# Moving GpSimd's two multiplies of the decayed C ahead of the first rotation sum

## The reference

```python
Bm = _rms(Braw, B_norm_w)[:, :, None, :] + B_bias      # per head
Cm = _rms(Craw, C_norm_w)[:, :, None, :] + C_bias
tc = jnp.cumsum(theta, axis=1)
cos_t, sin_t = (jnp.cos(tc), jnp.sin(tc))
def rope(v):
    v1, v2 = (v[..., :N // 2], v[..., N // 2:])
    return jnp.concatenate([v1 * cos_t - v2 * sin_t, v1 * sin_t + v2 * cos_t], -1)
Bm, Cm = (rope(Bm), rope(Cm))
def step(carry, inp):
    h, prevBx = carry
    x_t, B_t, C_t, a_t, g_t, b_t = inp
    Bx = jnp.einsum('bhp,bhn->bhpn', x_t, B_t)
    h = a_t[..., None, None] * h + g_t[..., None, None] * Bx + b_t[..., None, None] * prevBx
    y = jnp.einsum('bhpn,bhn->bhp', h, C_t)
    return ((h, Bx), y)
```

## Time and profile before

| what | value |
|---|---|
| median of 3 runs | 1266.17 us (1259.84 to 1267.21) |
| the profiled execution | 1261.08 us, of which its span is 1259.3 us |
| DVE busy | 1185.8 us, 94% |
| PE busy | 1121.2 us, 89% |
| ACT busy | 820.9 us, 65% |
| POOL busy | 766.8 us, 61% |
| mean granted TensorE clock | 0.963 |

### The profile page before, as it was taken

One profiled execution on the slowest core, in us unless ns is written; L12 is line 12 of the kernel. 1 busy time (PEld: TensorE's weight loads), 2 busy tenths in 40 slices (PEclk: granted clock), 3 DMA queues, 4 the chain that ended last, 5 costly groups with the idle time before them and its releaser, 6 DMA issues. The chain is left out here.

```text
span 1259.3 us, 30431 instructions
## 1 busy us (share of the span) xinstructions
PE 1121.2 (89%) x11442; PEld 819.0 (65%) x11442; DVE 1185.8 (94%) x1795; ACT 820.9 (65%) x1270; POOL 766.8 (61%) x594
## 2 busy tenths in 40 slices
PE   3876489999999999999999999999999999999996
PEld 3753266667667667667666766666776676676665
DVE  7899489999999999999999999999999999999994
ACT  4677256666766676667666666667666666667663
POOL 4002146766766667666776676666766676767664
PEclk9875589999999999999999999999999999999999
DMA  8534554433544454445544364446443554433440
GB/s 188 194 100 100 133 118 120 116 88 92 145 119 102 109 128 113 101 99 135 128 119 95 86 146 113 102 109 135 111 104 96 131 127 120 97 86 94 113 102 26
DMA packets 91888, 142.94 MB, mean 114 GB/s; under 512 B 19326, under 2 KB 38591, under 8 KB 91327
## 3 DMA queue, kind: packets, MB, share of 16 engines
q1 hardware_dynamic: 91743, 141.00, 45.9%
HBM read 58.68 MB, written 13.37 MB: 57 GB/s over the span
## 5 line engine op out<-in xcount | busy, mean ns | idle before, releaser
L1477 POOL TENSOR_TENSOR rot<-part 128x512 f32<-128x512 f32 x256 | 383.2, 1497 | 362.0 <-DVE part L1274 362.0
L1274 DVE SCALAR_TENSOR_TENSOR part<-bcs,k_prmT,k_trig 128x512 f32<-128x512 f32 x512 | 565.1, 1151 | 18.4 <-DMA bcs<-bc_t 15.5
L1408 ACT ACTIVATE E<-d 128x512 f32<-128x512 f32 x256 | 151.9, 594 | 170.5 <-PE d L1102 170.2
L1486 POOL TENSOR_TENSOR ce<-rot,eb 128x512 f32<-128x512 f32 x128 | 182.2, 1444 | 0.0
L1292 DVE TENSOR_TENSOR M<-s,E 128x512 f32<-128x512 f32 x256 | 163.5, 678 | 2.4 <-PE s L1113 1.8
L1113 PE MATMUL s<-rot 64*128 64x128 f32 x2048 | 149.7, 285 | 14.0 <-POOL rot L1477 13.9
L1113 PEld LDWEIGHTS s<-rot 64*128 64x128 f32 x2048 | 126.5, 188 | 51.2 <-issue 50.7
L1530 POOL TENSOR_TENSOR sqa<-sqa,sq 128x512 f32<-128x512 f32 x112 | 142.6, 1273 | 16.2 <-ACT sq L1418 7.8
L1087 PE MATMUL r<-k_w_zx,xns 128*128 128x256 f32 x512 | 134.7, 387 | 15.0 <-DMA xns<-xn_t 13.8
L1413 ACT COPY xk<-r 128x512 f32<-128x512 f32 x128 | 74.9, 588 | 103.0 <-PE r L1087 102.9
L1210 PE MATMUL y<-M,xk 128*64 128x128 f32 x2048 | 140.1, 279 | 0.0
(11 more groups left out here) (254 smaller groups left out, 1686.4 us busy)
## 6 DMA issues: line engine op xcount, KB each, us to landing
k_trig<-k_tri SPq DMA_DIRECT2D x512, 128.0 KB, 2.9
eb<-ecum_rows SPq DMA_DIRECT2D x128, 256.0 KB, 4.7
bcs<-bc_t SPq DMA_DIRECT2D x16, 256.0 KB, 3.9
bcs<-bc_t SPq DMA_DIRECT2D x32, 128.0 KB, 3.8
a_big<-in_L_attn_u SPq DMA_DIRECT2D x4, 512.0 KB, 6.1
xn_t<-a_xnT SPq DMA_DIRECT2D x1, 2048.0 KB, 11.4
tc_t<-a_tcT SPq DMA_DIRECT2D x1, 2048.0 KB, 15.9
bc_t<-a_tmp SPq DMA_DIRECT2D x1, 2048.0 KB, 8.0
```

What stands on the lines that cost most here:

```text
L1274: nc.vector.scalar_tensor_tensor(out=part[:, 2 * p + f, :], in0=bcs[:, (t + q // NQ) % 2, 2 * w + f, :], scalar=col, in1=trig[:, p, 1 - f, ...
L1408: nc.scalar.activation(E[:, h % 2, :], Dp[:], ACT.Exp).then_inc(e_ready, 1)
L1477: nc.gpsimd.tensor_tensor(rot[:, q % 2, p, w, :], part[:, 2 * p, :], part[:, 2 * p + 1, :], ALU.add).then_inc(rot_ready, 1)
L1486: nc.gpsimd.tensor_tensor(ce[:, p, :], rot[:, q % 2, p, 1, :], eb[:, p, :], ALU.mult).then_inc(ce_ready, 1)
```

## The change

In each round GpSimd runs the two `ce` multiplies of the current group first and then sum 0 of the next group, where it ran sum 0 first and the multiplies second. Sums 1 to 3 stay where they were. No instruction is added or removed, no wait is changed, and the other engines' programs are the same.

```diff
             for t in range(NS):
                 for q in range(NQ):
-                    if live(t, q + 1):
-                        sums(t, q + 1, 0)
                     c_decayed(t, q)
                     if live(t, q + 1):
-                        for k in range(1, 4):
+                        for k in range(4):
                             sums(t, q + 1, k)
```

## The result

The changed kernel takes 1229.97 us (median of 4 runs, 1226.61 to 1233.43) where the kernel before takes 1263.01 (4 runs, 1258.47 to 1267.21). The ratio is 0.9743, with a 95% interval of 0.9712 to 0.9774: faster by 33 us. The forecast was 1217 in a range of 1206 to 1244. The direction held, and about two thirds of the forecast saving of 49 us came. The profiled execution took 1226.61 us.

The account below looks back on a forecast made before the run. The prediction took VectorE, 94% busy, as the bound, with TensorE close behind. Savings by kind of round, less late spreads, came to 48.5 us: 1261.1 to 1212.6 for the profiled execution, 1217 from the median, range 1206 to 1244.

Parts of the forecast that it names:

- What bounds the kernel, and the port: VectorE leads, TensorE follows; rotations and GpSimd products can't run together, costing C 0.07 and D 1.02 us under `ce`.
- What leaves, and where `ce` goes: C and D become free, 1.09 us less a round; `ce` follows the second `sqa`, costing B 0.19 with odd t.
- a release counted by starts alone: Timing GpSimd by instruction starts would hold rotation B some 0.15 us longer, 3 us over odd-t rounds; the forecast decided against it.
- What waits behind the moved work: Sum 0 now follows both `ce` but is done 2.3 us before rotation E; `eb` keeps some 13 us of slack.
- What is late next: TensorE's work fits VectorE's new rounds by 0.04 and 0.07 us; ScalarE's sines and the spreads also come close.
- The forecast's own sign of being wrong: D still long, VectorE waiting for `k_trig` or `rot`, or rounds at TensorE's length above 16.1 us with VectorE idle.
- Rounds q = 2: Seven rounds with t > 0: `ce` and sum 0 behind `so` and `res`, C loses 0.64; saving 0.45 each, 3.2 us.
- Late spreads: Spreads landing late for rotation A: bounded by 0 and 0.3 us a round, taken as 0.1 over 42 rounds, minus 4.2 us.
- The rival that stops the saving at the spreads: Sines, spreads, rotation A and the z matmul bind the round: 27 us saved in 42 rounds, 8 elsewhere, 1231 us; chance 0.16.
- Rounds q = 0 and 1: Seven rounds each, D already free: q = 0 saves 0.48 each, 3.4 us; q = 1 saves 0.55 each, 3.9 us.
- ordinary even rounds: 23 ordinary rounds with even t save 1.09 us each, 25.1 us.
- ordinary odd: 19 ordinary rounds with odd t save 0.90 us each, 17.1 us.

Follow-up runs that it names:

- e7: Kernel before the change with the `ce` multiplies left out after the first group, semaphore still raised: 1009.9 us for the 62 rounds, ratio 0.9667.
- e6: Changed kernel with one `ce` multiply ahead of sum 0 and the other behind it: 1016.9 us for the 62 rounds, ratio 0.9712.
- e5: Changed kernel with `ce` moved right behind sum 3 of the same group, ahead of both `sqa`: 1040.9 us for the 62 rounds, ratio 0.9871.
- e9: Changed kernel with GpSimd's eight products dealt two to each stretch without a VectorE rotation: 1024.6 us for the 62 rounds, ratio 0.9764.
- e11: e9 with the second `ce` (q = 3 to 7) waiting for rotation A, `so` and `res` back behind round q = 1's squares: 1210.13 us, ratio 0.9595.
- e10: Changed kernel with only ScalarE's second square moved ahead of the second `E`: 1018.5 us for the 62 rounds, ratio 0.9698.
- e2: Changed kernel with each ScalarE square moved ahead of the `E` of the same place: ratio 1.0400.

## Why the prediction was right, and where its sum was not

*What bounds the kernel, and the port.* Right. VectorE's rotations were long because of GpSimd's products, and for no reason of their own: C and D are 0.74 with `ce` gone from under them, moved or left out (e7). "They wait for each other on semaphores only", in the section on the chip, is too strong for this kernel. The Trainium skill's page "SBUF — State Buffer", section "Who interferes with whom", says that a VectorE instruction with two SBUF inputs contends with a GpSimd instruction that reads SBUF, and that the one that comes second blocks. The rows here agree in both directions (B 0.94 behind `ce`, the first `ce` 1.7 behind A), and `hs`, with one of its two tensors in SBUF, lost nothing.

*What leaves, and where `ce` goes.* Right to 0.02 us where nothing else binds: the four odd rounds q = 3 take 15.91, and were forecast at 15.91. B's 0.19 showed as 0.20, with even t as 0 to 0.01; a release counted by starts alone would have made it some 0.34.

*What waits behind the moved work.* Right: no wait for `eb`, and sum 0 was never late for E.

*What is late next.* Here the sum failed, and the mechanism of the new bound was not in the forecast. I compared TensorE's work with VectorE's round and found that both fit, and I looked for rings through the sines and the spreads. I took A's 0.33 as fixed ("F and H lose as much ... A 0.33 to the second `sqa`"), because the second `sqa` follows sum 3 and so VectorE. It does that only while ScalarE's squares are early, and they stand behind an `E` that waits for TensorE. The slack there, 0.69 us (odd) and 0.90 (even), could have been read from the kernel before. With VectorE's round shorter by 0.9 us, the first square became the later of the two, and TensorE's schedule came back to VectorE through GpSimd's port: TensorE - `E` - square - `sqa` - A. It cost 0.43 us in 15 odd rounds (6.5 us) and 0.2 in 22 others (4.4). The forecast's own sign of being wrong, rounds above 16.1 us with VectorE idle, came by half: the rounds are at 16.17 and 16.32, but the wait lies inside A. e6 and e7 shorten this ring by B's wait and the rounds follow; in e5, e9 and e11 nothing ahead of A waits for a square, and they fall to between 15.76 and 16.07.

*Rounds q = 2.* The term with the wrong sign: forecast +3.2 us, measured -3.9. Two steps failed. The two `ce` were put at 612.08 and 613.31, as if nothing held the first, while rotation B, held by `res`, runs just there. The first `ce` took 1.73 us, 0.46 more, and with it C loses 1.08 and not 0.64, so the 3.2 us are nothing; the old order in these rounds gives the same (1020.8 against 1020.9). The 3.9 us are A's, by the ring above, with the wait of the second `M`.

*Late spreads.* Over-sized: forecast 4.2 us; VectorE's wait for `k_trig` went from 2.6 to 3.3 us. The step before it was right: the sines didn't move, and SyncE's spreads waited for them 55 times and 26.2 us in all (7 times and 6.3 us before). The rival that stops the saving at the spreads gave nearly the measured time, 1231, but not by its mechanism: its 27 us would have shown as VectorE idle before A.

*Rounds q = 0 and 1.* 4.0 and 3.1 us against 3.4 and 3.9: the sizes are right together, though q = 1 splits into 0.81 with odd t and nothing with even t, where B is held 0.9 us by the second `ce`; the split version frees it, and those rounds fall from 17.00 to 16.47.

The forecast's terms and their failure in one line, in us: ordinary even rounds 25.1 against 19.5, ordinary odd 17.1 against 10.7, q = 0 to 2 10.5 against 3.2, late spreads, taken off at 4.2, nearly nothing.

Even rounds close their ring at 16.16 although their `hs` chain is longer. By the rows they do so because two differences nearly cancel: from A to the second `xc` they take 5.38 us against 5.12 in odd rounds without B's wait (e6), but TensorE's part, with fewer y matmuls, takes 6.31 against 6.53. No run changes either alone.

## What to carry to other kernels

A record of VectorE that is longer than its twins may hold a wait, as here: lay GpSimd's timeline beside it, and if the two meet, count it as a wait that can be moved. When a wait is taken from the leading engine and the next one is less than a microsecond behind, follow each instruction that shares something with the leader to the engine that releases it, and read its slack; a port that two engines share closes rings that no wait of the leader shows. In a ring of four engines, place another engine's short work by the gaps of the engine that leads, two products to a gap here. Letting that engine wait on purpose so as not to start just ahead of the leader made rounds even and was part of the fastest version, but its own worth is small here.

## What the runs showed of the hardware that I had not expected

- GpSimd can stand idle 1.58 us on purpose in each ordinary round of the fastest version, which has 16 us less in all than the changed kernel, by the whole new order of its products.
- Two `sqa`, the second of which reads what the first wrote, start 1.41 us apart, two `ce` 1.23. The gap is the same in e10, where the second square is there before the first `sqa` ends, so the sooner second square won nothing in ordinary rounds.
- With each square ahead of its `E` (e2) TensorE idled 1.6 to 2.3 us a round in pieces, and its granted clock was 0.98 on average between 600 and 1100 us of the span, where the changed kernel has 1.00. Two rounds of e2 (t=4 q=5 and q=6, columns as in the earlier trace rows) give the price:

```profile
829.47:848.30 18.83, 17.03 (x174) 12.94 (x174) 15.90 (x27) 11.30 (x18) 11.45 (x9) 0.91 0.37 81
848.30:865.62 17.32, 15.52 (x174) 11.72 (x174) 15.82 (x27) 11.30 (x18) 11.45 (x9) 1.00 0.44 98
```

TensorE is idle for 1.80 us in both, and for 1.80 in the round ahead of them. By the clock of 0.91, 3.4 us of the first ran at the lower level, 1.2 GHz, and it is 1.5 us longer. No run shows why one of two such rounds falls and the other doesn't.
